# Rotary projections of a two-layer hybrid block: the partner half copied across partitions instead of projected a second time

## What is computed

```python
def _layernorm(x, eps=1e-05):
    m, v = jnp.mean(x, -1, keepdims=True), jnp.var(x, -1, keepdims=True)
    return (x - m) / jnp.sqrt(v + eps)
# x: (16, 512, 256) float32; 16 heads of 16
x = x + attn_a(_layernorm(x), ...)     # linear attention with a causal running state and 4 memories
x = x + ffn(_layernorm(x), ...)        # 256 -> 1024 -> 256, ternary weights, relu
x = x + attn_b(_layernorm(x), ...)     # softmax attention with rotary embedding, below
x = x + ffn(_layernorm(x), ...)        # the same ffn again

def attn_b(x):
    q = (x @ W_Q.T).reshape(B, S, 16, 16)
    k = (x @ W_K.T).reshape(B, S, 16, 16)
    v = (x @ W_V.T).reshape(B, S, 16, 16)
    q, k = rope(q), rope(k)            # y_even = cos*x_even - sin*x_odd; y_odd = sin*x_even + cos*x_odd
    scores = einsum('bhqd,bhkd->bhqk', q, k) / 4, causal, softmax over k
    return (attn @ v) @ W_O.T
```

## Time and profile before

| | us |
|---|---|
| median of three runs | 2647.59 (2646.87 to 2655.3) |
| the profiled execution's own time | 2646.55 |
| its span | 2644.8 |
| PE busy | 2151.8 (81%) |
| DVE busy | 1723.8 (65%) |
| ACT busy | 1308.6 (49%) |
| POOL busy | 970.2 (37%) |

### The profile page before, as it was taken

One profiled execution on the slowest core, in us unless ns is written; L12 is line 12 of the kernel. 1 busy time (PEld: TensorE's weight loads), 2 busy tenths in 40 slices (PEclk: granted clock), 3 DMA queues, 4 the chain that ended last, 5 costly groups with the idle time before them and its releaser, 6 DMA issues.

```text
span 2644.8 us, 54601 instructions
## 1 busy us (share of the span) xinstructions
PE 2151.8 (81%) x18402; PEld 1414.8 (53%) x18402; DVE 1723.8 (65%) x4346; ACT 1308.6 (49%) x2630; POOL 970.2 (37%) x852
## 2 busy tenths in 40 slices
PE   0567979888897988889898988989798888988676
PEld 0435555655565565555555555555555555655333
DVE  6637766667676667767666776667676676766241
ACT  1333645646464554646455464636546364644423
POOL 2434252533425253342525344242534324252201
PEclk9878999989898999989999999989999999999878
DMA  2313233333232333323133333313333332223030
GB/s 91 49 28 58 52 49 57 49 65 57 42 53 46 57 52 70 50 54 53 34 57 58 65 49 65 53 34 52 59 57 49 66 57 42 52 46 49 17 49 9
DMA packets 121770, 135.68 MB, mean 51 GB/s; under 512 B 16912, under 2 KB 102544, under 8 KB 121488
## 3 DMA queue, kind: packets, MB, share of 16 engines
q1 hardware_dynamic: 110736, 115.08, 27.8%
q10 hardware_dynamic: 10752, 16.78, 1.7%
HBM read 80.95 MB, written 41.94 MB: 46 GB/s over the span
## 4 chain that ended last, share of the span: by engine, by line
issue 48%; POOL 18%; PE 17%; DVE 8%; ACT 5%; DMA 2%; SPq 1%; POOLq 0%; ACTq 0%; DVEq 0%
PE bank L1252 6%; POOL place L603 5%; POOL place L593 5%; POOL place L614 3%; POOL rstd L578 2%; POOL bsl L618 2%; PE bank L1397 2%; PE bank L1206 2%; ACT place L670 2%; POOL place L639 1%; ACT place L700 1%; ACT place L703 1%; PE bank L1265 1%; PE bank L1310 1%; DVE stats L898 1%
## 5 line engine op out<-in xcount | busy, mean ns | idle before, releaser
L1139 DVE TENSOR_REDUCE mxs<-bank 128x1 f32<-128x128 f32 (+3 forms) x1024 | 428.5, 482 | 199.5 <-PE bank L1399 199.2
L803 ACT ACTIVATE place<-bank 128x512 f32<-128x512 f32 (+1 forms) x768 | 352.0, 548 | 254.4 <-PE bank L1413 253.4
L603 POOL TENSOR_TENSOR place<-am,place 128x512 f16<-128x512 f32 x256 | 290.5, 1156 | 274.1 <-ACT place L715 266.1
L578 POOL TENSOR_TENSOR rstd<-ve,halfc 128x4 f32<-128x4 f32 x64 | 64.9, 1015 | 615.7 <-DVE ve L905 615.7
L715 ACT ACTIVATE place<-am 128x512 f16<-128x512 f32 x256 | 149.5, 624 | 283.6 <-DVE am L964 283.6
L1411 PE MATMUL bank<-qst,kst 128*128 128x512 f16 (+3 forms) x1024 | 239.3, 304 | 41.6 <-DMA qst<-nmt 25.8
L1265 PE MATMUL bank<-w2q,place 128*128 128x256 f16 x2048 | 253.0, 276 | 20.6 <-POOL place L593 17.4
L1397 PE MATMUL bank<-kst,qst 96*128 96x128 f16 (+3 forms) x1024 | 240.7, 306 | 23.8 <-DMA kst<-scratch 10.8
L964 DVE SCALAR_TENSOR_TENSOR am<-bank,tri 128x512 f32<-128x512 f32 x256 | 167.1, 685 | 102.4 <-PE bank L1282 63.2
L1265 PEld LDWEIGHTS bank<-w2q,place 128*128 128x128 f16 x2048 | 197.3, 99 | 61.5 <-issue 26.1
L1206 PE MATMUL bank<-ident,place 128*128 128x128 f32 x512 | 101.1, 336 | 149.8 <-ACT place L670 146.3
(11 more groups left out here) (159 smaller groups left out, 4634.9 us busy)
## 6 DMA issues: line engine op xcount, KB each, us to landing
scratch<-place SPq DMA_DIRECT2D x128, 256.0 KB, 2.3
qst<-scratch SPq DMA_DIRECT2D x256, 128.0 KB, 5.4
kst<-scratch SPq DMA_DIRECT2D x256, 128.0 KB, 6.0
xa<-x SPq DMA_DIRECT2D x16, 512.0 KB, 3.6
xc<-xb ACTq DMA_DIRECT2D x16, 512.0 KB, 2.9
out<-xc ACTq DMA_DIRECT2D x16, 512.0 KB, 4.4
qst<-wall SPq DMA_DIRECT2D x8, 256.0 KB, 8.2
qst<-nmt SPq DMA_DIRECT2D x128, 4.0 KB, 1.7
```

Of the source, the lines that this page charges most:

```text
L603: G.tensor_tensor(alp[:, n % 2, k, :], am[:, k, :], ahp[:, n % 2, k, :], ALU.subtract).then_inc(s["al"], 1)
L803: A.activation(pf[h % SLOTS][:, S2_COL[k]:S2_COL[k] + S2_W[k]], bank_of(L2, ("S2", h, k))[:, 0:S2_W[k]], ACT.Exp, scale=D ** -0.5 / RS ** ...
L1139: V.tensor_reduce(mxs[:, g:g + 1], bank_of(L2, ("S1", n, k))[:, Q_AT[i]:Q_AT[i] + (i + 1) * P], AX, ALU.max).then_inc(s["mx"], 1)
```

## The change

The numbers of `MARKS` are new in both lanes, and `CUT` is 7 where it was 5. Of the table one row is shown; the rest of the diff comes to this:

```diff
-AQ, AK, AV, AO, BQ, BK, BV, BO, BQR, BKR = range(10)
+AQ, AK, AV, AO, BQ, BK, BV, BO = range(8)
+PAIR = P // 2
-LANDED = 2 * 4 * 16
-CUT = 5
+LANDED = {1: 2 * 4 * 16, 2: 2 * 4 * 2 * 16}
+CUT = 7
 MARKS[2]["pe"]
-            "PB": [14.5, 19.6, 23.2, 28.9],
+            "PB": [9.9, 11.4, 13.5, 17.8],
-        t12 = L2.place4
+        t12 = L2.place2[:, 0:8 * S].bitcast(F32).rearrange("p (n r s) -> p n r s", n=2, r=2)
 stack(L, half, t), SP
                     for dst, part, which in ((L.qst, q_part, 0), (L.kst, k_part, 1)):
-                        sp.dma_start(dst[to, heads, :], L.scratch[half, part, :, which, :]
-                                     .rearrange("(h d) s -> d h s", d=D)).then_inc(L.landed[half], 16)
+                        rows = L.scratch[half, part, :, which, :]
+                        if L is L1:
+                            sp.dma_start(dst[k * D:(k + 1) * D, heads, :],
+                                         rows.rearrange("(h d) s -> d h s", d=D)).then_inc(L.landed[half], 16)
+                            continue
+                        for r in range(2):
+                            to = slice(k * D + r * D // 2, k * D + (r + 1) * D // 2)
+                            sp.dma_start(dst[to, heads, :], rows.rearrange("(r h i) s -> r i h s", r=2, h=HH8)[r]
+                                         ).then_inc(L.landed[half], 16)
 lane2, POOL
-                    pool.wait_ge(s["t12"], due(L2, "t12", t, 2 * q + 2))
-                    G.tensor_tensor(L2.sq[:, q, :], t12[:, 0, :], t12[:, 1, :], ALU.add).then_inc(s["y"], 1)
+                    pool.wait_ge(s["xs"], due(L2, "xs", t, 2 * q + 2))
+                    G.tensor_tensor(t12[:, q % 2, 1, :], t12[:, q % 2, 1, :], sint[:, :], ALU.mult).then_inc(s["t2"], 1)
+                    pool.wait_ge(s["t1"], due(L2, "t1", t, q + 1))
+                    pool.wait_ge(s["t2"], due(L2, "t2", t, q + 1))
+                    G.tensor_tensor(L2.sq[:, q, :], t12[:, q % 2, 0, :], t12[:, q % 2, 1, :],
+                                    ALU.add).then_inc(s["y"], 1)
 lane2, ACT
+                        act.wait_ge(s["pr"], due(L2, "pr", t, q + 1))
+                        for r in range(2):
+                            to, of = slice(r * PAIR, (r + 1) * PAIR), slice((1 - r) * PAIR, (2 - r) * PAIR)
+                            A.activation(t12[to, q % 2, 1, :], bank_of(L2, ("PB", q))[of, :], ACT.Copy,
+                                         scale=RS / WS).then_inc(s["xs"], 1)
 lane2, DVE
-                    for r in range(2):
-                        dve.wait_ge(s["pr"], due(L2, "pr", t, 2 * q + r + 1))
-                        V.scalar_tensor_tensor(t12[:, r, :], bank_of(L2, ("PB", q, r))[:, :], RS / WS,
-                                               (cost, sint)[r][:, :], ALU.mult, ALU.mult).then_inc(s["t12"], 1)
+                    dve.wait_ge(s["xs"], due(L2, "xs", t, 2 * q + 2))
+                    V.scalar_tensor_tensor(t12[:, q % 2, 0, :], bank_of(L2, ("PB", q))[:, :], RS / WS, cost[:, :],
+                                           ALU.mult, ALU.mult).then_inc(s["t1"], 1)
 lane2, PE
-                    project(L2, ("PB", q, 0), a, m, "pr", t)
-                    project(L2, ("PB", q, 1), b, m, "pr", t)
+                    project(L2, ("PB", q), mat, m, "pr", t)
```

More of the change, by code:

```diff
@@ L133 @@
+            "FTT": [24.2],
+            "UP": [28.1, 29, 30, 30.9, 33, 34.8, 36.6, 38.3],
+            "DN": [38.4, 46.8],
+            "DM": [40.5, 40.6, 40.9, 41.1, 41.4, 41.6, 42.7, 43.8],
+            "TT": [67.6],
+            "PA": [74.9, 78.6, 80.9, 83.1],
+            "V": [88.6, 92.3],
+            "SK": [93.8, 94, 94.2],
+            "RM": [96.9],
+            "ST": [97.1, 97.3, 98.3, 99.1, 100.3, 100.8],
         },
@@ L239, in jobs2 @@
     jobs = [(("T", 0, k), "xl", k + 1) for k in range(KH)]
-    jobs += [(("PB", t, r), "t12", 2 * t + r + 1) for t in range(4) for r in range(2)]
+    jobs += [(("PB", t), "t1", t + 1) for t in range(4)]
     jobs += [(("V", j), "vh", j + 1) for j in range(2)]
@@ L444, in sequence @@
             return of[bass.ds(t, 1)].rearrange("o p j f -> p (o j) f")
-        w_stage = [L1.qst, L1.kst]
-        w_stage = [t[:, :, :].rearrange("p a b -> p (a b)").bitcast(F32) for t in w_stage]
+        w_stage = L1.qst[:, :, :].rearrange("p a b -> p (a b)").bitcast(F32)
         f_stage = L2.qst[:, :, :].rearrange("p a b -> p (a b)").bitcast(F32)
@@ L469, in _ @@
             sp.dma_start(b2bc[:, :], b2.broadcast_to([P, H])).then_inc(c_in, 16)
-            sp.dma_start(cost[:, :], cos).then_inc(c_in, 16)
-            sp.dma_start(sint[:, :], sin).then_inc(c_in, 16)
+            for table, of in ((cost, cos), (sint, sin)):
+                for r in range(2):
+                    sp.dma_start(table[r * PAIR:(r + 1) * PAIR, :],
+                                 of.rearrange("(n r) s -> r n s", r=2)[r]).then_inc(c_in, 16)
             sp.wait_ge(pool_const, 1)
@@ L1269, in stacks_landed @@
             def stacks_landed(L, half, t):
-                pe.wait_ge(L.landed[half], (t + 1) * LANDED)
+                pe.wait_ge(L.landed[half], (t + 1) * LANDED[L.n])
             def products(n, t):
```

216 lines of the change are left out of this document (111 added, 105 removed), and 20 rows, old and new, of the table MARKS.

## The result

The changed kernel takes 2718.88 us (median of 4 runs), against 2650.27 us for the kernel before, run beside it: a ratio of 1.024, with a 95% interval of 1.020 to 1.029. It is slower, as forecast, but by 69 us and not by 211; the time lies inside the range and at the number of rival B (2730). The profiled execution took 2718.8 us, with a span of 2717.1.

The account below looks back on a forecast made before the run. PE, busy 81%, was taken as the engine to free; late loads make a passage 15.2 + 1 - 3.6 = 12.6 us longer. Fourteen give +176, with +10, +16 and +9 together +211 on 2646.55: 2857 us, range 2650 to 2940.

Parts of the forecast that it names:

- rival B: Lane 2's stack loads: loads to neighbouring eights overlap, a half takes 4 us more, a passage 4.6; 2730 us, chance 0.13.
- ahead of the loop: Two tiles moved over the loop's branch are done alone there, 4.5 us each: +9 us.
- beside sequence 14: Sequence 14 beside lane 1's end: a passage's 12.6 us less 3 for two tiles fewer, +10 us.
- the last sequence: Last sequence alone: first load to second scores goes from 23.4 to 39.4 us, +16 us.
- Loads of 8 partitions: Lane 2's stack loads: rate follows the partitions written, so a half's transfer takes 17.1 us, 8 more.
- The next step: From first load to second scores in a passage: 8 us more in each of two stretches, second scores 15.2 us later.
- Ahead of the stores: Before the first stores: 2.1 us kept from projections less rope chain, 1.5 from the order; gain 3.6 us a passage.
- The issues: SP issuing a half's sixteen loads: 0.47 us each, 7.6 in all, less than the transfer, so no cost.
- the clock: PE's clock after the longer wait, granted at 0.70 of full: 1 us more a passage.
- A: Rival: lane 2's loads keep their pace at 103 GB/s, -81 us, 2566 us; chance 0.17.
- C: Rival: loads keep pace but the rope chain on ACT and POOL eats the gain; 2650 to 2660 us, chance 0.03.
- D: Rival: worse than the sum, clock low longer or issues held up by full queues; above 2940 us, chance 0.05.

Follow-up runs that it names:

- e12: Kernel before, with the stack's four blocks laid in turn, so each of lane 2's 16-partition loads writes partitions four apart; theory 2610 to 2670 us, came as its theory says.
- e6: e3 with the stack's blocks reordered, so a half is three loads of 32 partitions and two of 16: 2563.6 us.
- e10: e3 put back to the kernel before's order (its old table of marks and the cut at tile 5): 2685.7 us.
- e8: Changed kernel put back to the kernel before's order (its old table of marks and the cut at tile 5): 2768.8 us.
- e3: Changed kernel with columns laid feature by feature across heads, so a half is eight loads of 16 partitions again: 2613.7 us.
- e2: Kernel before with lane 2's loads issued as 16 a half, each still 16 partitions wide but of 4 heads instead of 8: 2650.2 us, ratio 1.000.
- e11: Kernel before with each keys' load going two blocks (32 partitions) on from the queries' load it follows: 2646.1 us.
- e14: Kernel before with each keys' load going one block (16 partitions) on from the queries' load it follows: 2647.6 us.
- e9: Changed kernel with each keys' load going two blocks (32 partitions) on from the queries' load it follows: 2709.1 us, ratio 1.022 or 1.024.
- e15: Changed kernel with each keys' load going one block (16 partitions) on from the queries' load it follows: 2708.9 us, ratio 1.022 or 1.024.
- e16: e3 with the stack's blocks laid in turn, so its 16-partition loads write partitions four apart: 2562.5 us.
- e1: Kernel before with only lane 2's 16-partition stack loads each issued as two of 8 partitions: 2799.9 us.

## Why the prediction was right in sign and wrong in size

The 72 us between the two spans lie so: 8.2 ahead of the loop (243.34 against 235.15 of the earlier trace rows; forecast 9), 55 in fourteen passages (forecast 176), 3 beside sequence 14 (forecast 10), 6 in the last sequence (forecast 16).

**The step that failed** is the term "Loads of 8 partitions", the sentence "I take 17.1, so 8 more". A half grew by 4.7 and 3.4 us in the loop (9.6 to 14.3, 9.8 to 13.2), and by 6.4 and 3.9 in the last sequence. The premise that the partitions written at a time bound the rate is right for loads that pile up, as e12 and e6 show. But the rate does not go on falling in proportion: a half moves 73 GB/s into 8 partitions, 9.2 for each, where it moved 109 into 16, 6.8 for each. In packets: eight engines with packets of 142 ns, as long as before, would need 128 x 0.142 = 18.2 us for a half's 1024 packets, close to the 17.1 that I took; with 114 they need 14.6, and 14.3 is measured. Why a packet is shorter stays open: it ranges from 87 to 130 ns between the passages of one execution, and in the five slowest first halves (15.7 to 16.0 us) the last eight landings come within 0.09 to 0.15 us of each other, in the fastest three (11.4 to 12.9 us) within 0.36 to 0.53. That fits engines that drift apart, so that some are already at the other eight partitions, and crowd each other less. But the second halves show it more weakly (15.3 to 15.6 us with 0.32 to 0.35), even the slowest first halves have 130 ns and not 142, and no run set the drift.

Two smaller points of the working. The rises of the earlier trace rows stand eight slices, 2.24 us, apart, and not 2.4; nothing rests on the difference. And the 9.9 us a half of the estimate by 54 GB/s go by a half of some 9.5 us; by the 9.1 of the sum they are 10.3, and the time about 2930.

The page of the Trainium skill cited ahead of the result, from which I estimated 54 GB/s for 8 partitions, was nearer to the changed kernel's slowest stretch (66) than to its mean (1.05 MB in 14.3 us is 73), and put the time too high as my term did.

**The next step had the right mechanism and passed the error on.** Two halves follow each other, and both are in the second scores: first load to second scores (the first load is issued 2.7 us behind the first stores) is 30.2 us for 24.5, so 5.7 more; forecast 15.2. Of the halves' 8.1 us, 2.4 are lost on the way. I had allowed 0.8. The rest is that in the kernel before the loads were not the last to come: its second half had landed by 43.2 (33.4 + 9.8), as the maxima were issued (43.1), and e12 shortened the loads there by 2 to 3 us for nothing.

**Ahead of the stores** 2.4 us were gained (18.2 to 15.8); forecast 3.6. By e10 the projections less the rope chain are 0.6 of it, where I had 2.1, and the order 1.8 (e8 to after), where I had 1.5. The copies take 591 ns and POOL's multiply 1269, as estimated from the earlier trace rows, but POOL's add behind it became slower, 1495 for 1283:

```profile
L651 POOL TENSOR_TENSOR place<-place 128x512 f32<-128x512 f32 x64 | 95.7, 1495 | 17.5 <-DVE place L1156 10.5
L648 POOL TENSOR_TENSOR place<-place,sint 128x512 f32<-128x512 f32 x64 | 81.2, 1269 | 101.3 <-ACT place L797 101.3
L797 ACT ACTIVATE place<-bank 64x512 f32<-64x512 f32 x128 | 75.7, 591 | 50.4 <-PE bank L1250 46.9
...
L1156 DVE SCALAR_TENSOR_TENSOR place<-bank,cost 128x512 f32<-128x512 f32 x64 | 43.5, 679 | 5.6 <-ACT place L797 5.5
```

**What I had not priced** is the order's other half. It puts the second half's stores at 25.3 us behind the hand-over for 30.7, and with it e8 and e10 show 3.9 and 4.3 us a passage. With wide loads the second half's loads follow at 31.6 us for 35.3 (e3, e10), which is most of the 4.3. With narrow ones they wait for the first half's, 34.8 for 37.3 (after, e8), and 1.8 of these 2.5 are the earlier start; the rest of the 3.9 I have not traced.

**The issues** cost nothing, as said (e2), at 0.35 us rather than 0.47. What is left of a passage, and what I had called **the clock**, is 0.6 us for 1 forecast (3.9 = 5.7 - 2.4 + 0.6; the means of the passages, which add up better than medians, give 6.1, -2.5 and 0.3). This is a rest and not a measured price of the clock: the mean granted clock fell from 0.926 to 0.894 of full, and what that costs within the other terms no run shows.

**The rivals.** B's number came out (4 us more a half, as it said, and 3.9 a passage for its 4.6). Its reason, that loads to neighbouring eights overlap, has no support in e11 and e14, where loads of 16 gained nothing from a next load that writes elsewhere, and e9 and e15 do not test it, since narrow loads alternate between the eights anyway. The drift above, if it is real, would be a form of it; so whether B was right or lucky is open. A did not happen; e6 and e16 show that its 2566 is there for loads that cost nothing. C's mechanism, a rope chain that adds up, is there in the old order (e8, e10: 15.0 us from stores to stores for 12.5), but whether it eats the gain is open (e10 is slower than the kernel before, e8 faster than e1). D stayed away.

## What to carry to other kernels

Before a change of layout that makes a DMA's partition range narrower, look at what the transfer now waits for: how many engines it keeps busy (the DMA share) and how long one packet takes, and not the rate alone, since both move together; and look at the pace of the issues, since even e2's packets to sixteen neighbours were short (56 ns) until the loads piled up. Rows of a contracted stack may stand in any order, so one can spread each load over partitions four apart, or make it 32 wide, and look at the issues' price (0.35 to 0.70 us) along with the packets. And a change that moves the work ahead of a transfer is judged together with its order: with wide loads the same change was 1.5% slower in the old order and 1.6% faster in the new.

## What the runs showed of the hardware

- Loads of 1 KB packets moved 103 to 116 GB/s into sixteen neighbouring partitions once they had piled up, 180 into 32 neighbours, 196 into sixteen that are four apart (there the issues are the limit), and 66 to 92 into eight neighbours (1.05 MB in 16.0 to 11.4 us).
- A 1 KB packet took 142 ns with sixteen engines on sixteen neighbours (e2's first four loads, issued 64 KB at a time: 56, at 143 GB/s), 114 with eight engines on eight neighbours, and 50 to 56 in the spaced layouts, where the issues are the limit.
- SP's issue of a load of 8 neighbouring partitions takes 0.35 us, of 16 neighbours 0.46, of 8 spaced ones 0.70 and of 16 spaced ones 0.64. e3's loads of 16 neighbours, whose rows follow one another in `scratch`, take 0.64 as well, so the spacing is not the only thing that makes an issue dear.
- Stores queued behind narrow loads begin early. In the slice view of 890 to 904 us of the changed kernel the rate rises to 301 GB/s just after the second half's stores are issued, falls back while narrow loads still run, and the stores' last part lands after them:

```profile
GB/s 0 0 0 99 158 99 82 85 56 102 61 97 70 79 85 70 99 59 97 70 88 88 190 287 261 301 114 100 73 85 91 82 102 59 105 70 97 79 120 155
```
